# Cross-attention on one core: key differences behind the last maximum, transposed maxima behind the run of values

## The reference

```python
def _lora_linear(x, W, A, B):
    return x @ W + SCALING * (x @ A @ B)
q = _lora_linear(hidden_states, Wq, Aq, Bq).reshape(bsz, q_len, NH, HD)
k = _lora_linear(traces, Wk, Ak, Bk).reshape(bsz, t_len, NKV, HD)
v = _lora_linear(traces, Wv, Av, Bv).reshape(bsz, t_len, NKV, HD)
...
scores = jnp.einsum('bhqd,bhtd->bhqt', q, k) / jnp.sqrt(jnp.asarray(HD, q.dtype))
attn = jax.nn.softmax(scores, axis=-1)
context = jnp.einsum('bhqt,bhtd->bhqd', attn, v)
...
out = _lora_linear(context, Wo, Ao, Bo)
return hidden_states + out
```

## Time and profile before

| | us |
|---|---|
| median of 3 runs | 1052.14 (1052.12 to 1054.42) |
| the profiled execution | 1053.82 |
| its span, first to last instruction | 1051.8 |
| PE busy | 973.5 (93%) |
| PEld busy | 802.1 (76%) |
| DVE busy | 583.5 (55%) |
| ACT busy | 433.4 (41%) |
| POOL busy | 320.3 (30%) |
| mean granted TensorE clock | 0.965 of full speed |
| q1, SP's DMA queue | 110.16 MB, 40.8% of 16 engines |

### The profile page before, as it was taken

The page is one execution under the profiler, slowest core; times in us unless marked ns, Lnnn a source line. Parts: engine busy times, 40 slices in busy tenths (PEclk is TensorE's granted clock), DMA queues, the critical chain, the costliest instruction groups (busy, mean ns, idle before and its releaser), DMA issues.

```text
span 1051.8 us, 15943 instructions
## 1 busy us (share of the span) xinstructions
PE 973.5 (93%) x5904; PEld 802.1 (76%) x5904; DVE 583.5 (55%) x1005; ACT 433.4 (41%) x843; POOL 320.3 (30%) x276
## 2 busy tenths in 40 slices
PE   6989999938899999999999999999999757989998
PEld 5879999937788787887887887877878534768886
DVE  5661221336677676676676676677667643333331
ACT  3341221302555555556556555565556433201000
POOL 1201000000335345355354453453543445300000
PEclk9999999969999999999999999999999767989999
DMA  6729523352251642542543444344243441466652
GB/s 194 232 82 247 169 75 105 108 141 60 71 123 44 143 113 48 136 110 68 116 111 89 94 111 107 76 110 117 68 114 83 111 122 51 136 223 198 197 162 80
DMA packets 106004, 124.73 MB, mean 119 GB/s; under 512 B 30048, under 2 KB 89568, under 8 KB 105936
## 3 DMA queue, kind: packets, MB, share of 16 engines
q1 hardware_dynamic: 102076, 110.16, 40.8%
q10 hardware_dynamic: 3860, 13.67, 3.5%
HBM read 87.59 MB, written 29.82 MB: 112 GB/s over the span
## 4 chain that ended last, share of the span: by engine, by line
PE 73%; DVE 12%; issue 4%; DMA 4%; ACT 3%; SPq 1%; POOL 0%; ACTq 0%; DVEq 0%; POOLq 0%
PE ps L686 10%; PE ps L687 10%; PE ps L688 10%; PE ps L877 8%; PE ps L892 8%; PE ps L865 7%; PE ps L826 5%; PE ps L828 4%; PE ps L830 4%; PE ps L771 4%; DVE maxima L1263 4%; DVE k_stack L1192 3%; PE ps L927 2%; DMA q_scratch<-q_out_lo 2%; DMA out_dram<-residual 1%
## 5 line engine op out<-in xcount | busy, mean ns | idle before, releaser
L1263 DVE TENSOR_REDUCE maxima<-ps 112x1 f32<-112x375 f32 x512 | 269.3, 542 | 92.9 <-PE ps L877 84.4
L1055 ACT ACTIVATE probs<-ps 125x448 f32<-125x448 f32 x384 | 207.8, 543 | 169.0 <-PE ps L865 168.1
L666 POOL TENSOR_TENSOR prob_sum<-probs 125x448 f32<-125x448 f32 x128 | 146.4, 1159 | 351.9 <-ACT probs L1055 350.4
L877 PE MATMUL ps<-k_stack,q_stack 96*112 96x376 f32 x512 | 185.7, 363 | 36.3 <-DVE maxima L1263 20.0
L865 PE MATMUL ps<-q_stack,k_stack 97*125 97x448 f32 x384 | 147.2, 384 | 11.6 <-DVE a_stack_o L1141 4.3
L672 POOL TENSOR_TENSOR prob_sum<-prob_sum,probs 125x448 f32<-125x448 f32 x128 | 147.5, 1159 | 26.2 <-ACT probs L1055 24.6
L877 PEld LDWEIGHTS ps<-k_stack,q_stack 96*112 96x112 f32 x512 | 92.2, 180 | 60.4 <-DVE maxima L1263 41.6
L826 PE MATMUL ps<-wv_hi,ct_hi 128*125 128x256 f32 x384 | 112.1, 292 | 0.1
L830 PE MATMUL ps<-wv_hi,ct_lo 128*125 128x256 f32 x384 | 109.1, 284 | 0.0
L828 PE MATMUL ps<-wv_lo,ct_hi 128*125 128x256 f32 x384 | 109.0, 284 | 0.0
L1186 DVE TENSOR_TENSOR ct_lo<-ps,ct_hi 128x375 fp32r<-128x375 f32 x128 | 70.2, 548 | 55.3 <-ACT ct_hi L992 55.3
(11 more groups left out here) (80 smaller groups left out, 1423.7 us busy)
## 6 DMA issues: line engine op xcount, KB each, us to landing
ctx_in<-in_ctx_dram SPq DMA_DIRECT2D x16, 1344.0 KB
q_stack<-q_scratch SPq DMA_DIRECT2D x96, 224.0 KB, 5.9
x_in<-in_x_dram SPq DMA_DIRECT2D x8, 896.0 KB, 8.8
q_scratch<-q_out_hi SPq DMA_DIRECT2D x16, 448.0 KB, 2.8
q_scratch<-q_out_lo SPq DMA_DIRECT2D x16, 448.0 KB, 3.8
attn_scratch<-attn SPq DMA_DIRECT2D x32, 224.0 KB, 4.2
attn_rows<-attn_scratch SPq DMA_DIRECT2D x14, 512.0 KB, 4.8
inv_tile<-inv_scratch SPq DMA_DIRECT2D x56, 128.0 KB, 4.8
```

Source lines behind the costliest of these rows:

```text
L877: mm = pe.matmul(ps[0:NQ, NAT + i % 2, 0:NTE], qst[nxt][0:STK, g, rr * NQ:(rr + 1) * NQ], kst[nxt][0:STK, g, :], start=True, stop=True)
L1055: act.activation(probs[:, c, j, :], ps[0:TR, score_bank(i), 0:QH], ACT.Exp, scale=SM).then_inc(exp_done, 1)
L1263: dve.tensor_reduce(maxima[:, h, i:i + 1], ps[0:NQ, NAT + i % 2, 0:NT], AX.X, ALU.max).then_inc(max_done, 1)
```

## The change

Three numbers of `PLAN` move. The four F0 were due with the E0 from 0.53 on, and are now due at 0.81; M goes from 0.805 to 0.82, so behind P at 0.815; E1 and F1 go from 0.82 to 0.83, which keeps them behind M.

```diff
-    + [("N", i, 0.02 + 0.045 * i) for i in range(JH * RH)] + [("M", 0, 0.805)]
-    + [(f"{kind}0", j, 0.53 + 0.045 * j) for kind in "EF" for j in range(JH)]
-    + [(f"{kind}1", j, 0.82) for kind in "EF" for j in range(JH)],
+    + [("N", i, 0.02 + 0.045 * i) for i in range(JH * RH)] + [("M", 0, 0.82)]
+    + [("E0", j, 0.53 + 0.045 * j) for j in range(JH)] + [("F0", j, 0.81) for j in range(JH)]
+    + [(f"{kind}1", j, 0.83) for kind in "EF" for j in range(JH)],
```

## The result

The changed kernel takes 1069.38 us in the median, the kernel before 1052.13 us in the same comparison: a ratio of 1.0163, 95% interval 1.009 to 1.0236. The median is 6.6 above the 1062.8 forecast and inside the range of 1056 to 1073. Its four executions lie in pairs, and the mean granted clock of each goes with its time: 1064.34 and 1064.12 at 0.965 and 0.968, 1075.03 and 1074.43 at 0.957. So the median lies between the pairs, where no execution was, and the two longer ones lie outside the range. The profiled execution is one of the shorter ones.

What follows compares the result with a forecast made beforehand. The prediction took TensorE as the bound, three quarters of the span, waiting for VectorE's maxima in each K tail. Terms 8.5 - 3.7 + 5.4 + 0.5 = +10.7 us on the median 1052.1 gave 1062.8, range 1056 to 1073.

Steps and rivals of the forecast that it cites:

- The borders, +8.5: K-to-V borders: P starts 1.58 us sooner, but waits at S.1 and N.2 lose 2.14; +0.6 each, times 14.
- The V-to-K border, 0: M and P change places at no cost; den_rows' load goes later but lands about when the reciprocal needs it.
- the bound of 3: Upper bound for the V-to-K borders if the reciprocal waits for its load: 13 x 0.2 = +3 us.
- Ahead of the loop, -3.7: Step making batch 1's keys: M 2.2 us sooner without two waits, plus 1.5 from products no longer at 1.2 GHz.
- The bound of -2.2: Ahead of the loop: the smaller gain, in us, if the clock falls anyway.
- Weight block 5, +5.4: Last steps: the maxima's DMA goes 5.5 us late on SP's queue, delaying block 5's loads and VectorE's sum; +5.4 us.
- Weight block 2, +0.5: One border before the last steps: a 2.9 us shift meets block 2's loads; between 0 and 2.9, taken as +0.5.
- rival 1: The clock falls at the borders, 1.5 us each: 1070 if in a third, 1084 if in all; chance 0.20.
- Rivals 2 to 4: 2: chain behind M fits, 1032, 0.07; 3: border gain and loss cancel, 1054.3, 0.08; 4: block 5 early, 1059.5, 0.08.

Runs made afterwards that it cites:

- e1_first: The changed kernel, but with E1 and F1 ahead of M, which stays behind P; 1040.76 us, ratio 0.9899 against the kernel before.
- again_a: The changed kernel unaltered, six timed executions; median 1070.40 us, ratio 1.0164 against the kernel before; its profiled execution 1066.36.
- again_b: The changed kernel unaltered, a single execution with a profile; 1066.06 us.
- again_c: The changed kernel unaltered, another single execution with a profile; 1075.14 us.
- before_a: The kernel before, unaltered, a single execution with a profile; 1048.91 us.
- before_b: The kernel before, unaltered, another single execution with a profile; 1049.39 us.
- tail_m_first: The changed kernel, but M stays ahead of P in the two halves of batch 14; 1062.54 us, ratio 1.0126 against the kernel before.
- m_only: The kernel before with only M moved behind P, E1 and F1 behind it, F0 unmoved; 1089.38 us, ratio 1.036.
- f0_only: The changed kernel with M back ahead of P, so only F0 moves; 1033.79 us, ratio 0.9826 against the kernel before.

## Why the prediction was right, and where it wasn't

**The borders, +8.5: right, a little small.** +0.70 a border, 9.8 in 14. (The figures of the prediction make 2.14 - 1.58 = 0.56 a border, 7.8 in 14; the 8.5 was rounded up.) Each link came as added up. P starts 1.44 us sooner against the half's start (1.59 predicted); S.1 waits 0.95 (1.05) and goes out at 6.19 (6.11); N.2 goes out at 7.54 (7.56). The difference to +0.6 lies in the gain, 0.15 smaller, not in the chain; 0.09 of it stands between K1.7's last product and P (0.26, 536.02 to 536.28, for 0.17). The last exp, said to end 0.9 behind S.11's issue, ended 1.13 behind it, since an E0 copy stood before it on ScalarE; whether P waited for it is not shown. That the chain is what I took it for is shown by e1_first: without E1 behind M the border gains 1.29 instead of losing 0.70. The wait of 0.9 at N.2 prints as 0.53; the place of N.2 agrees, so the rest lies between instructions, where the profile prints no idle time.

**The V-to-K border, 0: nearly right.** TensorE's list of waits has nothing for it, but the load of den_rows landed up to 4.3 us behind its issue, not 3.3, and where the reciprocal waited for it the K half grew by 0.24 and 0.28: 0.5 in this execution, 0.3 in again_a, none in again_b, 0.2 in again_c. That is inside the bound of 3.

**Where the terms lie, over all profiled executions.** Starts of rows subtracted; M's DMA is the one near 241 us, ahead of the loop.

| stretch, us | before, before_a, before_b | after, again_a, again_b, again_c |
|---|---|---|
| M's DMA to the sum of block 0 | 585.1, 584.3, 583.6 | 592.8, 592.7, 593.9, 600.4 |
| block 0 to block 2 | 9.16, 8.55, 8.90 | 10.95, 10.51, 10.45, 10.42 |
| block 4 to block 5 | 6.10, 7.29, 5.66 | 11.90, 11.77, 11.04, 11.83 |
| block 5 to the last P | 41.6, 38.3, 39.0 | 39.3, 38.7, 38.7, 39.4 |
| last P to the end | 145.9, 144.5, 145.9 | 143.4, 144.6, 144.4, 145.8 |

**Ahead of the loop, -3.7: the step that failed.** It was right at the place it was reckoned for, and wrong as a gain that stays. The product of L696 comes 3.6 us sooner. But 1.5 of that was the low clock behind M's wait, and in before_a and before_b the clock did not fall there: from the M of the step ahead to L696 those took 20.24 and 20.22, the first profile 21.78, the changed kernel 18.06. Only 2.2 are there in every execution. Nor did the 1.5 stay in the profiled pair: the clock of the changed kernel falls a little later, behind L696, and over 255 to 275 us its mean is 0.83 in the first profiles of both kernels. From the maxima's DMA near 241 us to the first P of the loop the kernel before took 43.8, 43.1 and 42.3, the changed one 41.3, 41.3, 41.3 and 40.0 (again_c): 2.5 between the first profiles, 1.7 on average without again_c, and 2.1 to 2.5 between executions with a like clock in that window (0.83 in before, before_a and the first three of the changed kernel, 0.91 in before_b and again_c). The bound of -2.2, "if the clock falls anyway", was the better figure. The first row of the table then adds up: it grows by 8.3 on average, without again_c and without the 1.5 of again_b's fall, for 9.8 at the borders, 0.3 at the reciprocals and 1.7 less.

**Weight block 5, +5.4: right.** The table's averages give 5.3, profile against profile 5.8; the loads landed 5.5 to 6.5 us behind their issue (5.8 assumed), and the maxima's DMA went just ahead of attn_rows1's load as described. tail_m_first shows the cause. The Trainium skill (DMA: Bandwidth & Descriptors, Anatomy of one DMA) gives its formula for DMAs that GpSimd issues, which the prediction left out, and my estimate of 2.3 us by it is for one of the block's four loads. These four, issued by SP behind other transfers, took 5.5 to 6.5; by that estimate the term would have been +1.5.

**Weight block 2, +0.5: under-sized.** It lost 1.8 us, 1.7 on average. What failed here is "these loads wait anyway behind the denominators' copy, which does not move": the sum of block 2 waited 2.91 us for its transfer. The later DMA does reach them: with M ahead of P in tail_m_first VectorE stands idle 0.30 there, as in the kernel before.

**Why the profiled pair still agrees to 0.2.** +10.7 against +10.5 is partly luck. The first three rows of the table sum to 7.7 + 1.8 + 5.8 = 15.3 between the two first profiles; the last two rows take 2.3 + 2.5 off again, because the profiled execution of the kernel before was slower there than before_a in both, and than before_b in the first, and the changed kernel's was its shortest at the end. That is a difference of executions, not of kernels: on average the last two rows differ by 0.6 and 0.9.

**The median, 6.6 above the forecast.** It grew by 17.3 us against the kernel before, not by 10.7. Two things make it. First, the terms: the growth that stays is 8.3 + 1.7 + 5.3 = 15.3 by the table, and fastest against fastest execution it is 15.2 (1047.2 and 1062.4). Of the 4.6 more than forecast, 2.0 are the gain ahead of the loop (1.7 and not 3.7), 1.3 the borders and 1.2 weight block 2. Second, rival 1 happened, in part: in again_c the clock falls at six of 14 borders, just over the "third of the borders" of that rival, at 1.55 a fall for the 1.5 assumed. That the 1074 to 1075 executions of the first comparison are of this kind is an inference from their mean clock, 0.957 where again_c has 0.955; they have no profile. That the median still falls inside the range owes something to luck: it lies between two executions inside and two outside, and no run tells how many of each kind to expect (again_a's six have a median of 1070.40). The chance of 0.20 treated rival 1 as something that either is so or isn't; it is so in a share of the executions, and that share belonged into the forecast. The description in the Trainium skill (TensorE: Matmul & The Clock Gate, A second HAM failure mode) agrees in kind, short waits between bursts and a clock that goes up and down; that it would be every border, as I read it, does not: it was none, none, one and six of 14.

**Rivals 2 to 4** are out: the chain doesn't fit (7.54 against the 7.0 at which it would decide), gain and loss don't cancel, and block 5 doesn't come early.

## What to carry to other kernels

Before an instruction that waits is moved behind a long run of another engine, list what stands behind it in its own engine's order and on its DMA queue; here the moved transpose was worth 0.19 us, and the copies E1 queued behind its negation cost 1.99 a batch, one DMA on SP another 7 in the last steps (1.7 and 5.3). A change of several moves is priced one by one: of these the move of F0 alone makes the kernel faster than both, 1033.79 us against 1048.96 before (0.9826), and the other takes away more than all of it. And where an engine's clock can fall behind a wait, one profile is not enough to price a new wait: the changed kernel with the same waits had no fall at its borders in two profiles, one in a third and six in a fourth.

## What the runs showed that was not expected

- **The same waits, another clock.** In again_c the six falls come at consecutive borders (stretches beginning at 543.6, 584.5, 625.5, 666.4, 707.4 and 748.4), with waits of 0.95 and 0.53 and the work between them as at the eight borders without one. In m_only they also numbered six, two or three borders apart, tail_m_first had two and again_b one. What decides whether a border has a fall is not shown by any run.
- **A shorter tail makes a transfer late.** In f0_only, at a period of 37.15, TensorE waits up to 1.4 us for the context's transfers, which were not late at 38.5 or 39.2 (300 to 820 us of the first profiles); in e1_first, at 37.22 with the maxima's DMA behind P, they are not late either. Why the order matters here was not tried.
